# Ten added transposes fewer, an earlier mask, a new order of attention steps 0 to 3, and other waits at the last scatters of a gated cross-attention and expert layer

## The reference, cut to what matters

```python
# x (4, 1024, 256), context (4, 77, 256), 16 heads of 16, 4 experts, top 2, inner width 688
def attention(q, k, v, mask):
    qh, kh, vh = heads(q @ w_q + b_q), heads(k @ w_k + b_k), heads(v @ w_v + b_v)
    s = einsum("bhqd,bhkd->bhqk", qh, kh) * D_HEAD ** -0.5
    s = where(mask == 0, -10000.0, s)
    return merge(softmax(s) @ vh) @ w_o + b_o

x = x + tanh(g_xattn) * attention(layernorm(x), context, context, mask)
xf = layernorm(x)
comb = top2_weights(softmax(xf @ gate_w.T))                 # two of four experts a row, renormalised
y = einsum("enh,ne->nh", experts(xf), comb)                 # silu(xf eg) * (xf eu), times ed
y = y + (silu(xf @ sg.T) * (xf @ su.T)) @ sd.T              # the shared expert
x = x + tanh(g_ffn) * y
```

## Time and profile before

| | |
|---|---|
| median of 3 runs | 918.8 us (918.7 to 919.09) |
| the profiled execution | 918.94 us |
| its span | 917.2 us |
| mean granted clock of TensorE | 0.99 |
| busy in the span: TensorE, VectorE, ScalarE, GpSimd | 883.0, 583.7, 474.2, 479.9 us |

### The profile page before, as it was taken

One profiled execution on the slowest core, in us unless ns is written; L12 is line 12 of the kernel. 1 busy time (PEld: TensorE's weight loads), 2 busy tenths in 40 slices (PEclk: granted clock), 3 DMA queues, 4 the chain that ended last, 5 costly groups with the idle time before them and its releaser, 6 DMA issues.

```text
span 917.2 us, 22259 instructions
## 1 busy us (share of the span) xinstructions
PE 883.0 (96%) x6671; PEld 789.5 (86%) x6672; DVE 583.7 (64%) x1294; ACT 474.2 (52%) x1794; POOL 479.9 (52%) x654
## 2 busy tenths in 40 slices
PE   8788899999999899999999999999999999999995
PEld 7566788888888799999989999999999999999994
DVE  5888899999998579778744444444444444444442
ACT  3988999999999334656532222222222222222221
POOL 4777667667656343675324444444444444444442
PEclk9899999999999999999999999999999999999998
DMA  7124223223312214232412222222222222222222
GB/s 210 40 74 137 89 79 110 84 66 91 97 59 82 94 46 131 90 108 89 147 36 40 40 40 40 36 44 34 46 34 41 39 40 40 39 41 35 45 34 24
DMA packets 56865, 61.74 MB, mean 67 GB/s; under 512 B 15643, under 2 KB 45184, under 8 KB 56800
## 3 DMA queue, kind: packets, MB, share of 16 engines
q1 hardware_dynamic: 42871, 43.15, 15.0%
q0 software_dynamic: 12864, 17.57, 12.0%
q10 hardware_dynamic: 1064, 0.21, 0.1%
HBM read 34.78 MB, written 25.82 MB: 66 GB/s over the span
## 4 chain that ended last, share of the span: by engine, by line
PE 83%; DVE 6%; ACT 4%; issue 3%; DMA 2%; POOL 1%; DVEq 0%; SPq 0%; POOLq 0%; ACTq 0%
PE p_s L346 27%; PE p_t L356 13%; PE p_f L2424 8%; PE p_f L370 5%; PE p_f L2469 4%; PE p_s L2424 3%; ACT prob L1238 3%; PE p_t L2355 3%; PE p_s L2341 3%; PE p_m L2382 2%; PE p_m L2370 2%; PE p_s L2469 2%; PE p_t L360 2%; PE p_m L2322 2%; PE p_m L331 2%
## 5 line engine op out<-in xcount | busy, mean ns | idle before, releaser
L211 POOL DMA_INDIRECT out_rows<-yout,add_at x67 | 107.2, 1601 | 195.7 <-DVE yout L289 192.9
L1238 ACT ACTIVATE prob<-p_s,negmax 128x77 f32<-128x77 f32 x512 | 161.6, 377 | 8.9 <-DVE negmax L1750 8.6
L296 DVE TENSOR_TENSOR hid<-p_s,sil 128x688 f32<-128x688 f32 x67 | 58.6, 875 | 163.2 <-ACT sil L249 139.0
L249 ACT ACTIVATE sil<-p_s 128x688 f32<-128x688 f32 x67 | 50.0, 746 | 193.6 <-PE p_s L346 193.6
L1238 ACT ACTIVATION_READ_ACCUMULATOR prob<-p_s,negmax 128x1 f32 x512 | 130.5, 259 | 0.0
L882 POOL TENSOR_TENSOR prob<-prob,rinv 128x616 f32<-128x616 f32 x64 | 79.2, 1247 | 64.6 <-DVE rinv L1757 64.6
L346 PE MATMUL p_s<-wgu_hi,fxT_hi 128*128 x402 | 110.7, 384 | 0.0
L346 PE MATMUL p_s<-wgu_lo,fxT_hi 128*128 x402 | 105.5, 371 | 0.0
L346 PE MATMUL p_s<-wgu_hi,fxT_lo 128*128 x402 | 105.5, 370 | 0.0
L260 ACT ACTIVATE hT_hi<-p_f 128x512 fp32r<-128x512 f32 x66 | 39.6, 600 | 122.6 <-PE p_f L370 122.6
L356 PE MATMUL p_t<-wd_hi,hT_hi 128*128 x330 | 98.3, 298 | 0.0
(11 more groups left out here) (287 smaller groups left out, 2456.0 us busy)
## 6 DMA issues: line engine op xcount, KB each, us to landing
xr<-in_x SPq DMA_DIRECT2D x16, 256.0 KB, 2.9
x_scratch<-xr SPq DMA_DIRECT2D x16, 256.0 KB, 2.7
xn_scratch<-xn SPq DMA_DIRECT2D x16, 256.0 KB, 2.1
xt_scratch<-xnT SPq DMA_DIRECT2D x16, 256.0 KB, 2.3
xin<-xt_scratch SPq DMA_DIRECT2D x16, 256.0 KB, 3.5
x1in<-x_scratch SPq DMA_DIRECT2D x16, 256.0 KB, 3.3
out_rows<-syout SPq DMA_DIRECT2D x16, 256.0 KB, 2.3
raw<-in_L_ffn_ed SPq DMA_DIRECT2D x4, 688.0 KB, 4.2
```

The lines of the kernel that those rows point to most:

```text
L211: pool.indirect_dma_start(out, bass.IndirectOffsetOnAxis(add_at[k][:, :], 0), yout[k][:, :], None, compute_op=ALU.add).then_inc(s_add, 16)
L249: act.activation(sil[:, :], p_gu[:, 0:FF], ACT.Silu).then_inc(s_sil, 1)
L296: nc.vector.tensor_tensor(hid[:, 0:FF], p_gu[:, FF:2 * FF], sil[:, :], ALU.mult).then_inc(s_hid, 1)
L1238: last = act.activation(prob[n % 2][t][:, m * PW + h * SK:m * PW + (h + 1) * SK], p_s[:, 2 * t + h // 4, col:col + SK], ACT.Exp, bias=negm ...
```

## The change

It has four places. On TensorE the added transposes after the context are 2 (before the first keys) and 4 (behind `x_T(0)`), in place of 4, 4 and 8. SyncE issues mask(0) before w_q, and VectorE makes the first blind mask ahead of `keys_lo`. `first_steps` of four engines holds nearly the same operations in another order (half-head splits of some `exps` move too). The next to last scatter takes the order of waits that the last one has.

```diff
--- before.py
+++ after.py
@@ -200,7 +200,7 @@
             wait(pool, s_add, 16 * (j - 1))
             pool.tensor_copy(add_at[k][:, :], slot_id[:, bass.ds(j, 1)]).then_inc(s_add_at, 1)
             pool.wait_ge(s_add_at, j + 1)
-            if isinstance(j, int) and j == NS - 1:
+            if isinstance(j, int) and j >= NS - 2:
                 pool.wait_ge(s_add, 16 * j)
                 settle(pool)
                 pool.wait_ge(s_yo, j + 1)
@@ -766,8 +766,8 @@
             load_x(0)
             sp.dma_start(ctx_sb[:, :, :], v["ctx_in"].rearrange("b k d -> k b d")).then_inc(s_ctx, 16)
             sp.dma_start(wk[:, :, :], v["w_k"].rearrange("(c p) d -> p c d", p=P)).then_inc(s_wk, 16)
+            load_mask(0)
             sp.dma_start(wq[:, :, :], v["w_q"].rearrange("(c p) d -> p c d", p=P)).then_inc(s_wq, 16)
-            load_mask(0)
             sp.dma_start(wv[:, :, :], v["w_v"].rearrange("(c p) d -> p c d", p=P)).then_inc(s_wv, 16)
             load_x(1)
             sp.dma_start(gw_sb[:, :], v["gate_w"]).then_inc(s_gw, 16)
@@ -998,45 +998,45 @@
 
             def first_steps():
                 rstd1(2)
+                normalise(0, 0)
+                normalise(0, 1)
                 normed_early(2)
                 residual_bias(0)
-                normalise(0, 0)
-                normalise(0, 1)
                 normalise(0, 2)
+                normalise(0, 3)
                 residual_bias(1)
-                normalise(0, 3)
-
+
+                residual_bias(2)
+                normalise(1, 0)
                 next_keys(1, 0)
-                residual_bias(2)
                 rstd1(3)
-                normalise(1, 0)
+                normed_early(3)
+                normalise(1, 1)
+                normalise(1, 2)
                 next_keys(1, 1)
-                normalise(1, 1)
-                normed_early(3)
-                normalise(1, 2)
                 normalise(1, 3)
 
-                next_keys(2, 0)
                 rstd2(0)
-                normalise(2, 0)
                 rstd1(4)
                 down_tail()
+                next_keys(2, 0)
+                next_keys(2, 1)
+                normalise(2, 0)
+                residual_bias(3)
                 normalise(2, 1)
-                residual_bias(3)
+                normalise(2, 2)
                 normed_early(4)
-                normalise(2, 2)
                 normalise(2, 3)
-                next_keys(2, 1)
 
                 rstd2(1)
+                rstd1(5)
+                normed_early(5)
                 normalise(3, 0)
                 xn_lo(0)
-                rstd1(5)
                 normalise(3, 1)
-                normed_early(5)
                 normalise(3, 2)
+                residual_bias(4)
                 normalise(3, 3)
-                residual_bias(4)
 
             def even_step(i):
                 n = (i - FIRST) // 2
@@ -1327,61 +1327,62 @@
 
             def first_steps():
                 exps(0, 0)
-                exps(0, 1, 0, HH // 2)
                 xT_copy(1)
+                exps(0, 1)
                 w_hi(0)
                 w_hi(1)
-                exps(0, 1, HH // 2)
+                q_hi(1)
+                exps(0, 2, 0, HH // 2)
                 other_keys_hi()
-                exps(0, 2, 0, HH // 2)
-                q_hi(1)
                 w_hi(2)
                 exps(0, 2, HH // 2)
                 exps(0, 3)
 
                 w_hi(3)
+                t_copy(0, 0)
+                exps(1, 0, 0, HH // 2)
+                t_copy(0, 1)
                 xT_copy(2)
-                t_copy(0, 0)
-                exps(1, 0)
+                exps(1, 0, HH // 2)
+                t_copy(0, 2)
+                exps(1, 1)
+                w_hi(4)
+                t_copy(0, 3)
                 q_hi(2)
-                t_copy(0, 1)
-                exps(1, 1, 0, HH // 2)
-                t_copy(0, 2)
-                exps(1, 1, HH // 2)
-                t_copy(0, 3)
-                w_hi(4)
-                exps(1, 2)
+                exps(1, 2, 0, HH // 2)
                 w_hi(5)
+                exps(1, 2, HH // 2)
                 exps(1, 3)
 
-                w_hi(6)
                 t_copy(1, 0)
                 exps(2, 0)
                 t_copy(1, 1)
+                w_hi(6)
                 xT_copy(3)
+                t_copy(1, 2)
                 exps(2, 1)
-                t_copy(1, 2)
+                t_copy(1, 3)
+                q_hi(3)
                 w_hi(7)
-                q_hi(3)
-                t_copy(1, 3)
                 exps(2, 2, 0, HH // 2)
+                xn_copy(0)
                 w_hi(8)
-                xn_copy(0)
                 exps(2, 2, HH // 2)
                 exps(2, 3)
 
                 lg_copy(0)
+                exps(3, 0, 0, HH // 2)
                 t_copy(2, 0)
-                exps(3, 0)
+                exps(3, 0, HH // 2)
+                exps(3, 1, 0, HH // 2)
                 t_copy(2, 1)
                 xT_copy(4)
-                exps(3, 1, 0, HH // 2)
+                w_hi(9)
                 t_copy(2, 2)
                 exps(3, 1, HH // 2)
+                q_hi(4)
                 t_copy(2, 3)
-                q_hi(4)
                 xn_hi(0)
-                w_hi(9)
                 w_hi(10)
                 xn_copy(1)
                 exps(3, 2)
@@ -1837,11 +1838,11 @@
             dve.wait_ge(s_bias, 48)
             dve.wait_ge(s_kps, 1)
             keys_T(p_s[:, 1, :], 0, 1)
+            no_sight(0)
             keys_lo(0, 1, 0)
             dve.wait_ge(s_own, 3)
             for m in range(KC):
                 key_hi(m)
-            no_sight(0)
             q_lo(0)
             stats_1(1)
 
@@ -1868,70 +1869,70 @@
                 context_values(1)
                 rest_of_start()
                 stats_1(2)
+                recip(0, 0)
                 half_max(0, 2)
-                recip(0, 0)
+                recip(0, 1)
                 w_lo(0)
-                no_sight(1)
-                recip(0, 1)
+                w_lo(1)
                 half_max(0, 3)
-                w_lo(1)
+                keys_lo(1, B, 1)
                 q_lo(1)
                 recip(0, 2)
+                no_sight(1)
                 w_lo(2)
-                keys_lo(1, B, 1)
 
                 half_max(1, 0)
+                recip(0, 3)
+                stats_1(3)
                 no_sight(2)
                 half_max(1, 1)
-                recip(0, 3)
+                w_lo(3)
                 recip(1, 0)
-                w_lo(3)
-                q_lo(2)
-                stats_1(3)
                 half_max(1, 2)
                 recip(1, 1)
+                w_lo(4)
+                q_lo(2)
                 last_t_copy(0)
                 half_max(1, 3)
+                w_lo(5)
                 recip(1, 2)
-                w_lo(4)
-                w_lo(5)
 
                 attention_out(0)
                 half_max(2, 0)
-                recip(1, 3)
                 stats_1(4)
                 attended(0)
+                recip(1, 3)
+                stats_2(0)
                 half_max(2, 1)
                 w_lo(6)
-                stats_2(0)
+                normed_2(0)
+                half_max(2, 2)
                 recip(2, 0)
-                half_max(2, 2)
-                normed_2(0)
+                q_lo(3)
                 w_lo(7)
-                q_lo(3)
                 last_t_copy(1)
                 half_max(2, 3)
+                w_lo(8)
+                no_sight(3)
                 recip(2, 1)
                 recip(2, 2)
-                no_sight(3)
-                w_lo(8)
 
                 attention_out(1)
                 half_max(3, 0)
-                no_sight(4)
                 recip(2, 3)
+                half_max(3, 1)
+                stats_1(5)
                 attended(1)
-                half_max(3, 1)
                 stats_2(1)
                 half_max(3, 2)
+                normed_2(1)
                 recip(3, 0)
-                normed_2(1)
-                stats_1(5)
                 q_lo(4)
                 w_lo(9)
+                recip(3, 1)
                 last_t_copy(2)
+                no_sight(4)
                 w_lo(10)
-                recip(3, 1)
                 half_max(3, 3)
                 recip(3, 2)
 
@@ -2556,13 +2557,12 @@
                                                 start=(k == 0), stop=(k == KC - 1))
                 last.then_inc(s_kps, 1)
 
-            keep_warm(4)
+            keep_warm(2)
             pe.wait_ge(s_ctxT, 1)
             pe.wait_ge(s_wk, 16)
             keys_of(0, 1, p_s[:, 1, :])
+            x_T(0)
             keep_warm(4)
-            x_T(0)
-            keep_warm(8)
             pe.wait_ge(s_wq, 16)
             q_T(0)
             pe.wait_ge(s_ctxT, 1 + KC)
@@ -2589,41 +2589,41 @@
                 values_of_context(0)
                 values_of_context(1)
                 x_T(1)
+                scores(0, 2)
                 w_T(0)
+                q_T(1)
```

(28 more changed lines are left out.)

## The result

In the first comparison the changed kernel took 912.63 us (median of 4 executions, 912.32 to 913.77), the kernel before 918.75 (4, 917.51 to 919.09): ratio 0.9938, 95% interval 0.9921 to 0.9955, 6.1 us faster, below the forecast range of 914.0 to 918.9. By the medians that is 3.2 us; the ratio is 0.9968, interval 0.9955 to 0.9980, so 1.8 to 4.1 us. Over all comparisons the kernel before has 113 executions, median 917.14, from 914.05 to 919.79, and the changed one 15, median 913.68, from 912.32 to 915.43.

The account below looks back on a forecast made before the run. Bound: a ring of three engines in attention steps 0 to 3, then a full TensorE stream from 101.60 us. Sum: 918.94 - 2.5 (0.9 + 1.6) - 0.2 = 916.2, set at 916.3; range 914.0 to 918.9.

Parts of the forecast that it names:

- (5): End of attention step 3: the product of probabilities and values runs at full clock, 3.57 - 1.93 = 1.6 us won.
- first scores sooner: Start: scores of step 0 begin near 15.5 us in place of 17.20, 1.7 us sooner, bounds 1.0 and 1.9.
- last scatters: End of kernel: older scatter's wait and a semaphore step pass before the rows come, 0.2 us won, bounds 0 and 0.75.
- The mask step: Start, VectorE: first blind mask moves into the wait for the high keys, taking 0.46 us; its 1.1 us hole closes.
- The transposes' 0.6: Start, TensorE: fewer added transposes let the first rows' transposes end at 10.9 us, before 11.56, 0.6 us sooner.
- near 9: Start: query weights, issued some 0.5 us later, land near 9 us and are wanted at 11.6, so covered.
- the cold query projection: Rival at the start: fewer transposes raise the pace later, q takes about 4 us for 1.97; 919.5 us, chance 0.04.
- (1, 2): Steps 0 and 1: low half of q(1) queues later; 0.7 of 1.7 us given back, then step 1's waits even out.
- Even: Step 1: one VectorE wait shrinks to nearly nothing, but the third maximum waits about 1.5 us for scores(1,2).
- (3): Probabilities times values of step 0: 3.64 us at the low clock, 1.93 at the high; this fall stays, nothing won.
- (4): Step 2: VectorE is full (14.76 of 16.00 us), same work in another order, plus or minus 0.3 us.
- a second fall stays: Rival, end of step 3: TensorE still drops to the low clock, 1.6 us not won; 917.7 us, chance 0.33.

Follow-up runs that it names:

- the repeated one: The changed kernel unaltered, run once more beside more executions of the kernel before: 913.85 us (11) against 917.05 (34).

## Why the prediction was wrong

The direction was right, the number was not. The forecast of 916.3 lies 3.7 us above the 912.63 measured. Of these, 1.8 are the level that it started from (918.8 for 917.05), 0.7 a gain that is larger than forecast (3.2 for 2.5), and 1.2 the draw of the four executions (912.63 for 913.85).

**The step that failed** is (5), the sum's term for step 3: "3.57 - 1.93 = 1.6 us" priced the faster product and nothing else, though its own text says that the longest wait ahead of it shrinks. The two profiles show 16.96 us become 15.50 ahead of the product and 18.73 become 17.22 from it on: 1.46 + 1.51 = 3.0 us. Undone it cost 3.0 (2.5 by the ratios), alone it gave 2.5 (1.8). Beside it failed the starting level. Term by term, in the two profiles of the first comparison:

| term | forecast us | read us |
|---|---|---|
| first scores sooner | 1.7 | 2.8 |
| given back up to the product of step 0 | -0.8 | -1.6 |
| from that product to step 2's (the fall, "left in place", and step 2) | 0 | 1.9 |
| step 3 | 1.6 | 3.0 |
| last scatters | 0.2 | 0.5 |

The terms add up to 2.7 forecast and 6.6 read, which is the difference of the two profiled executions (918.94 and 912.32). The third belongs to the execution and not to the kernel: in the second profile of the changed kernel it is 0.3. So does a part of the first, as the paragraph on the start says. (The forecast of 916.3 was also set 0.2 above 918.8 less the 2.7 of its own sum.)

**The level.** "918.94 (the profiled execution ...)", with a median "0.1 below", was taken as the kernel's time. Its 113 executions have median 917.14. There is one clear gap among them, from 917.91 to 918.70, with 32 executions above and 81 below; 30 of these lie under 916. The profile I reasoned from is one of the upper 32: slow keys and three falls of the clock, of which I named two (the other is from 31.4 to 34.7 us). I took three executions that agree to 0.4 us for a narrow kernel. That 2.7 forecast and 3.2 (1.8 to 4.1) measured lie close is in part luck: the terms behind them miss both ways.

**Start, 1.7 us forecast.** The mask step holds (1.2 us at equal pace in the first scores, 1.1 forecast). The transposes' 0.6 does not: at the fast pace they are worth nothing, as the query weights are waited for (0.86 us), which my landing "near 9" missed; they land near 10.4. At the slow pace 0.4 is seen. The 2.8 us between the two profiles are 1.2 of mask and about 1.6 of pace, and the pace belongs to the execution: the kernels with the old start show 15.46 to 15.78 with fast keys where the kernel before showed 17.20 with slow ones. What of it reaches the end is open: the mask alone gave 2.0 us by its ratio on the kernel before, the start undone in the whole cost 0.2 by the ratios and 0.6 by the medians on the changed one. Nor did the cold query projection come.

**Order.** (1, 2) "0.7 us given back" was the right sign; in the profiles it is 1.6 and 1.4. By the undone kernels (0.9968 against 0.9944 and 0.9950) the lists of steps 0 and 1 cost about 2 us. "Even" in (2) does not hold: the wait for scores(1,2), which I put at 1.5 us, was 2.35, and the maximum before it was late too. (3) The fall before the first values' product stays in most profiles (3.34 us in the second one of the changed kernel). In the first it is absent, the product takes 1.93 us, and the only fall is the one from 26 to 36.6 us. (4) Step 2 within 0.3: 0.4 measured, inside the spread. (5) Step 3: right in kind, half in size, as said. The rival "a second fall stays" is out: neither profile of the changed kernel has it.

**Scatter.** 0.2 forecast. The last scatter follows its rows 0.42 to 0.52 us sooner in nine of the twelve profiles that have the new waits, and 0.40, 0.32 and 0.05 sooner in the others, where 0.46 to 0.69 us lie between release and issue in place of 0.27 to 0.31; why there is not shown. My ground, that a transfer has its own time to start, holds for only 0.27 of the 0.75.

The parts do not add up. Alone on the kernel before, the four give 0.8, 2.0, 0.3 and 0.8 us by their ratios, 3.9 together, where the whole gives 2.9. The draw of the clock or an interplay of the lists may be the reason; these runs do not tell which.

**A version beyond both:** start, scatter, steps 2 and 3 of the changed kernel with steps 0 and 1 of the kernel before: 911.79 and 912.38 us in two comparisons, ratios 0.9950 and 0.9944.

## What to carry to other kernels

Three executions that agree do not bound a kernel whose clock is drawn anew each time: look for marks of the draw in the profile (here 1.83 or 1.09 us for the same eight matmuls) before taking its time as the level. Undo and do alone each part of an order: here one step's list was worth about 2 to 3 us and two others cost about 2, and the sum looked like one plain gain. When a wait ahead of a slow product shrinks, price the wait and the product both. A transpose that waits for another engine's late product should not stand ahead of matmuls that could run: here it cost 4.32 us of idle TensorE.

## What was not expected of the hardware

The granted clock in the windows reads 1.00 for the first 12 us in all profiles, while the same eight matmuls take 1.09 us in most, 1.83 in three (kernel before, transposes alone, scatter alone) and 1.91 without transposes: before its first change in the record it is no evidence of the pace. The 20 transposes at the start took 3.73 to 4.53 us in different executions, so the rise can come inside them. And falls of the clock differ between two executions of one kernel: one of the changed kernel has a single fall, the other two:

```profile
26.00:36.60 10.60, 8.96 (x37) 6.54 (x38) 8.34 (x19) 8.89 (x47) 8.53 (x8) 0.52 0.05 4
```

```profile
26.00:36.85 10.85, 9.46 (x39) 7.05 (x40) 8.35 (x19) 9.14 (x48) 8.70 (x9) 0.53 0.05 4
43.00:47.00 4.00, 4.00 (x39) 2.01 (x32) 2.38 (x6) 3.30 (x22) 3.05 (x3) 0.57 0.15 27
```

The first of these fences is the profile of the first comparison, the second that of the repeated one.
